# A four-layer decoder kernel: one DMA moved ahead of another in the L2 expert loop, weight loads split over two queues, the zeroing of buffer rows moved and cut

## The reference

```python
capacity = int(CAPACITY_FACTOR * T * K / E)
ranks = take_along_axis(cumsum(onehot, axis=0), flat_sel[:, None], axis=1)[:, 0] - 1
valid = ranks < capacity
slot = where(valid, flat_sel * capacity + ranks, sentinel)
padded = zeros((sentinel + 1, d)).at[slot].set(x_rep)
h = gelu(einsum('ecd,edf->ecf', padded, w1)); out_padded = einsum('ecf,efd->ecd', h, w2)
gathered = where(valid, out_padded[min(slot, sentinel - 1)], 0)
out = (gathered * weights).sum over the two choices
```

## Time and profile before

| | |
|---|---|
| median of three executions | 2066.54 us |
| the profiled execution's own time | 2069.29 us |
| its span, first to last instruction | 2067.6 us |
| PE busy | 1643.8 us (80%) |
| DVE busy | 911.0 us (44%) |
| ACT busy | 711.5 us (34%) |
| POOL busy | 436.8 us (21%) |
| moved by DMA | 37.63 MB, 18 GB/s over the span |

### The profile page before, as it was taken

One profiled execution on the slowest core, in us unless ns is written; L12 is line 12 of the kernel. 1 busy time (PEld: TensorE's weight loads), 2 busy tenths in 40 slices (PEclk: granted clock), 3 DMA queues, 4 the chain that ended last, 5 costly groups with the idle time before them and its releaser, 6 DMA issues. The chain is left out here.

```text
span 2067.6 us, 31792 instructions
## 1 busy us (share of the span) xinstructions
PE 1643.8 (80%) x11656; PEld 963.7 (47%) x11656; DVE 911.0 (44%) x2515; ACT 711.5 (34%) x1423; POOL 436.8 (21%) x517
## 2 busy tenths in 40 slices
PE   1899899994799998869899987136156999969998
PEld 1344434443444444545644435124042555548887
DVE  3455345533355654641256535311354555324444
ACT  1244424442176775524213444011041333422221
POOL 2534043400121110000053400320515434100000
PEclk8999999997999998969999998567576999969999
DMA  8200000000000000000040000011200000000000
GB/s 235 67 2 1 1 1 1 1 1 0 0 1 1 1 1 1 1 0 1 4 148 2 1 1 1 20 53 52 59 12 6 12 12 6 1 0 0 0 0 20
DMA packets 45933, 37.63 MB, mean 18 GB/s; under 512 B 3972, under 2 KB 40040, under 8 KB 45800
## 3 DMA queue, kind: packets, MB, share of 16 engines
q1 hardware_dynamic: 43752, 31.65, 5.1%
q0 software_dynamic: 2048, 4.20, 0.7%
HBM read 23.26 MB, written 12.58 MB: 17 GB/s over the span
## 5 line engine op out<-in xcount | busy, mean ns | idle before, releaser
L1309 ACT ACTIVATE scores_L_experts_L<-L3x_psL 128x512 f32<-128x512 f32 x128 | 76.4, 597 | 173.8 <-PE L3x_psL L1172 170.2
L1346 DVE CUSTOM_DVE_ANT_0 L3x_junk<-L3x_psS,L3x_mask_rows 128x256 f32<-128x256 f32 x224 | 86.4, 422 | 92.6 <-PE L3x_psS L1134 84.5
L1172 PE MATMUL L3x_psL<-identb,L3x_mask_parts 128*128 128x256 bf16 x768 | 96.2, 276 | 0.0
L2433 ACT ACTIVATE L3f_activated<-L3f_psG 128x512 f32<-128x512 f32 x72 | 43.0, 597 | 153.0 <-PE L3f_psU L2412 153.0
L2466 DVE TENSOR_TENSOR L3f_hidden<-L3f_activated,L3f_psU 128x512 f32<-128x512 f32 x72 | 49.6, 688 | 103.0 <-ACT L3f_activated L2433 103.0
L852 ACT ACTIVATE L0x_probs<-L0x_psL 128x512 f32<-128x512 f32 x96 | 52.1, 595 | 114.1 <-PE L0x_psL L665 78.9
L852 ACT ACTIVATE L2a_probs<-L2a_psL 128x512 f32<-128x512 f32 x96 | 52.1, 595 | 104.2 <-PE L2a_psL L663 69.4
L852 ACT ACTIVATE L0a_probs<-L0a_psL 128x512 f32<-128x512 f32 x96 | 52.1, 595 | 100.8 <-PE L0a_psL L663 65.0
L1154 PE MATMUL L3x_psL<-L3x_qm,ctx_T 32*128 32x512 f32 x256 | 73.7, 651 | 12.1 <-DVE L3x_mx L1346 11.6
L2398 PE MATMUL L3f_psY<-experts_L_L,L3f_hidden 128*128 128x128 f32 x576 | 76.9, 276 | 5.0 <-DVE L3f_hidden L2466 4.9
L1172 PEld LDWEIGHTS L3x_psL<-identb,L3x_mask_parts 128*128 128x128 bf16 x768 | 70.4, 98 | 21.5 <-issue 13.7
(11 more groups left out here) (768 smaller groups left out, 4025.8 us busy)
## 6 DMA issues: line engine op xcount, KB each, us to landing
packed_rows<-zeros SPq DMA_DIRECT2D x1, 4608.0 KB, 27.2
L2f_rows<-packed_rows SPq DMA_DIRECT2D x8, 320.0 KB, 3.6
unpacked_rows<-L2f_y SPq DMA_DIRECT2D x8, 320.0 KB, 2.7
experts_L_L<-in_L_ffn_w_dram SPq DMA_DIRECT2D x1, 2048.0 KB, 8.5
unpacked_rows<-zeros SPq DMA_DIRECT2D x1, 2048.0 KB, 25.1
scores_L_experts_L<-in_L_ffn_w_dram SPq DMA_DIRECT2D x1, 2048.0 KB, 7.9
L3x_mask_rows<-in_mask_Bx1xSxS_ff_dram SPq DMA_DIRECT2D x8, 256.0 KB, 2.7
experts_L_L<-n_L_ffn_expert_gate_dram SPq DMA_DIRECT2D x1, 1024.0 KB, 13.4
```

The source lines that it names most:

```text
L1172: last = nc.tensor.matmul(at[:, :, t * P:(t + 1) * P], parts[:, b % 2, i, t, u * P:(u + 1) * P], two, start=False, stop=i == PARTS - 1, sk ...
L1309: nc.scalar.activation(probs[:, half, a, k, :], psL[i % RING][:], ACT.Exp).then_inc(s_prob, 1)
L1346: last = nc.vector.tensor_tensor_reduce(out=junk[:, i, :], in0=psS[a][:, i * S:(i + 1) * S], in1=mrow[:, b % 2, t, :], scale=1.0, scalar=L ...
```

## The change

It has three parts.

1. In `slot_experts`, SP issues `load(c + 3)` ahead of the wait and store of pair c.
2. In `load_and_turn`, the loads are split: `x`, the LoRA weights, `ctx` with the int32 weights, and the rest on SP (28 DMAs); the square and router weights and four bias rows on ACT's queue (20 DMAs), ahead of ACT's copies. Four semaphores take the place of one: PE waits for the LoRA weights, then for the squares, then for `ctx`; DVE waits for `ctx`, and at its end for the rest. ACT alone copies out the first 23 transposed tiles; the last 25 are shared. The LoRA products come before the `ctx` tiles. The seven small DVE steps on index tables come before the wait for `ctx`.
3. The layer 1 expert loads and the zeroing leave this stage for SP in the L0a stage. 5120 rows of `packed` are zeroed instead of 9216, and none of `unpacked`. The gather uses new indices `home`: the slot, or row 0 where there is no room (its weight is 0). They cost one more DVE instruction for each of the two choices.

```diff
-SQUARE = ["L1_attn_Wq", ..., "L3_xattn_wo_w", "L0_attn_w_proj"]
+SQUARE = ["L0_attn_w_proj", "L1_attn_Wq", ..., "L3_xattn_wo_w"]
...
+        from_ctx = len(turns)
+        by_dve = [i >= from_ctx and i % 2 == 1 for i in range(len(turns))]
...
             def _(sp):
-                for dst, src in firsts:
-                    sp.dma_start(dst, src).then_inc(first, 16)
-                for dst, src in loads:
-                    sp.dma_start(dst, src).then_inc(loaded, 16)
-                for dst, src in late:
-                    sp.dma_start(dst, src).then_inc(w["late"], 16)
-                sp.wait_ge(zeros, 1)
-                sp.dma_start(w["packed"].rearrange("(a p) d -> p a d", p=P), w["zeros"][:].unsqueeze(1).to_broadcast([P, ROWS2 // P, D])
-                             ).then_inc(w["zeroed"], 16)
-                sp.dma_start(w["unpacked"][ROWS2 - 2 * B * S:, :].rearrange("(a p) d -> p a d", p=P),
-                             w["zeros"][:].unsqueeze(1).to_broadcast([P, 2 * NT, D])).then_inc(w["zeroed"], 16)
+                sp.dma_start(mem.x[:], dram["x"].rearrange("b (t p) d -> p (b t) d", p=P)).then_inc(first, 16)
+                for dst, src in lora_loads:
+                    sp.dma_start(dst, src).then_inc(s_lora, 16)
+                for dst, src in ctx_loads:
+                    sp.dma_start(dst, src).then_inc(s_ctx, 16)
+                for dst, src in rest:
+                    sp.dma_start(dst, src).then_inc(s_rest, 16)
...
             def _(pe):
-                pe.wait_ge(loaded, 16 * len(loads))
+                pe.wait_ge(s_lora, 16 * len(lora_loads))
                 for i, (src, dst) in enumerate(turns):
                     if i >= rings:
-                        j = i - rings
-                        pe.wait_ge((moved_act, moved_dve)[j % 2], j // 2 + 1)
+                        wait_moved(pe, i - rings)
+                    if i == lora_after:
+                        pe.wait_ge(s_square, 16 * len(square_loads))
+                    if i == from_ctx:
+                        wait_moved(pe, lora_after - 1)
+                        nc.tensor.matmul(lora[:, 0:3 * P], la_attn[:], lbT_attn[:], start=True, stop=True)
+                        nc.tensor.matmul(lora[:, 3 * P:4 * P], la_proj[:], lbT_proj[:], start=True, stop=True).then_inc(lora_done, 1)
+                        pe.wait_ge(s_ctx, 16 * len(ctx_loads))
...
             def _(act):
+                for dst, src in square_loads:
+                    act.dma_start(dst, src).then_inc(s_square, 16)
+                for dst, src in rest_act:
+                    act.dma_start(dst, src).then_inc(s_rest, 16)
                 for i, (src, dst) in enumerate(turns):
-                    if i % 2 == 0:
+                    if not by_dve[i]:
...
             def _(dve):
-                dve.wait_ge(loaded, 16 * len(loads))
+                dve.wait_ge(built, w["iotas"])
...
+                dve.wait_ge(s_ctx, 16 * len(ctx_loads))
...
 def quad_heads(...):
                     for dst, src in loads:
                         sp.dma_start(dst, src).then_inc(w["late"], 16)
+                    if clear:
+                        sp.dma_start(clear[0], clear[1]).then_inc(clear[2], 16)
...
 def slots_of_two(...):
                     steps.step(nc.vector.scalar_tensor_tensor(at[:], key[i][:], -float(capacity), rank[:], ALU.mult, ALU.add))
+                    steps.step(nc.vector.scalar_tensor_tensor(home[:, i, :], at[:, :, 0], float(E * capacity), fits[:, :, 0],
+                                                              ALU.add, ALU.mult))
...
 def slot_experts(...):
-                pool.wait_ge(w["zeroed"], 32)
+                pool.wait_ge(w["zeroed"], 16)
...
-                                                     bass.IndirectOffsetOnAxis(ap=slot[:, i, t:t + 1], axis=0)).then_inc(s_back[t // TPB], 16)
+                                                     bass.IndirectOffsetOnAxis(ap=home[:, i, t:t + 1], axis=0)).then_inc(s_back[t // TPB], 16)
...
                 for c in range(PAIRS):
+                    if c + 3 < PAIRS:
+                        load(c + 3)
                     sp.wait_ge(s_y, c + 1)
                     sp.dma_start(rows_of(unpacked, c), y[:, c % 2, :, :]).then_inc(s_store[c % 2], 16)
-                    if c + 3 < PAIRS:
-                        load(c + 3)
```

More of the change, by code:

```diff
@@ L200, in load_and_turn @@
         lora = ctx.enter_context(nc.psum_tensor("lora", [P, 4 * P], F32))
-        loaded, first, casts = sem("weights_loaded"), sem("x_loaded"), sem("dequantized")
+        first, casts = sem("x_loaded"), sem("dequantized")
+        s_lora, s_square, s_ctx, s_rest = (sem(n) for n in ("lora_loaded", "squares_loaded", "ctx_loaded", "rest_loaded"))
         built, turned, moved_act, moved_dve = sem("ident_built"), sem("turned"), sem("moved_by_act"), sem("moved_by_dve")
         lora_done, chain = sem("lora_done"), sem("prologue_chain")
-        lanes, zeros = sem("lanes"), sem("zeros_ready")
+        lanes = sem("lanes")
         lane, kind = sb("lane", [P, P], I32), sb("lane_kind", [P, 3, P], I32)
@@ L220, in load_and_turn, with wait_moved @@
         lora_after = 7
-        def square(n):
-            return dram[n]
-        firsts = [(mem.x[:], dram["x"].rearrange("b (t p) d -> p (b t) d", p=P))]
-        loads = [
+        by_dve = [i >= from_ctx and i % 2 == 1 for i in range(len(turns))]
+        act_total, dve_total = by_dve.count(False), by_dve.count(True)
+        def wait_moved(eng, i):
+            if by_dve[i]:
+                eng.wait_ge(moved_dve, by_dve[:i + 1].count(True))
+            else:
+                eng.wait_ge(moved_act, by_dve[:i + 1].count(False))
+        lora_loads = [
             (w_attn[:], dram["L0_attn_w_attn"].rearrange("(j p) d -> p j d", p=P)),
@@ L234, in load_and_turn @@
             (ffn_int[:, 2, :].rearrange("p (j d) -> p j d", d=P), dram["L0_ffn_w_up"].rearrange("(j p) d -> p j d", p=P)),
-            (wgq[:], dram["L1_xattn_Wgq"]), (wgk[:], dram["L1_xattn_Wgk"]),
+        ]
+        square_loads = [(nat[n][:], dram[n]) for n in SQUARE]
+        square_loads += [(wgq[:], dram["L1_xattn_Wgq"]), (wgk[:], dram["L1_xattn_Wgk"])]
+        square_loads += [(gate_nat[n][:], dram[n]) for n in gates]
+        rest_act = [(mem.bias[0:1, k:k + dram[n].shape[0] // P, :],
+                     dram[n].rearrange("(a j p) -> a j p", a=1, p=P)) for n, k in BIASES.items()]
+        rest = [(w["bias_cols"][:, c + j:c + j + 1], dram[n][j * P:(j + 1) * P].rearrange("(p a) -> p a", a=1))
+                for n, c in BIAS_COLUMNS.items() for j in range(dram[n].shape[0] // P)]
+        rest += [(w[n][:], dram[n]) for n in DIRECT]
+        rest += [
             (w["bgq"][:], dram["L1_xattn_bgq"].rearrange("(p a) -> p a", a=1)),
@@ L241, in load_and_turn @@
         ]
[L242 to L254 removed]
+        w["late_count"] = 0
         with nc.Block() as block:
@@ L287, in _ @@
                                                    fill=BIG, base=0, pattern=[[1, P]], channel_multiplier=-1))
-                steps.step(nc.gpsimd.iota(w["offset"][:], pattern=[[1, P]], base=P, channel_multiplier=-1))
                 tri = w["trinity"]
@@ L324, in _ @@
                 steps.step(nc.gpsimd.memset(mem.eps[:], EPS))
-                steps.step(nc.gpsimd.iota(w["desc_int"][:], pattern=[[-1, 16]], base=16, channel_multiplier=0))
-                steps.step(nc.gpsimd.iota(w["count_int"][:], pattern=[[1, GN]], base=1, channel_multiplier=0))
-                steps.step(nc.gpsimd.iota(w["token_int"][:], pattern=[[B * S, 2], [P, NT]], base=0, channel_multiplier=1))
                 steps.step(nc.gpsimd.memset(w["zeros"][:], 0.0))
-                pool.sem_inc(zeros, 1)
                 steps.step(nc.gpsimd.memset(w["nm"][:], 0.0))
@@ L385, in _ @@
                     steps.step(nc.vector.bn_aggr(mem.mv[:, t, :], mem.stats[:, t % 2, :]))
-                dve.wait_ge(loaded, 16 * len(loads))
+                dve.wait_ge(built, w["iotas"])
+                steps.step(nc.vector.tensor_copy(w["desc"][:], w["desc_int"][:]))
+                steps.step(nc.vector.tensor_copy(w["count"][:], w["count_int"][:]))
+                steps.step(nc.vector.tensor_copy(w["token"][:], w["token_int"][:]))
+                steps.step(nc.vector.tensor_scalar(w["slot_int"][:], lane[:, 0:1], GN - 1, None, ALU.bitwise_and))
+                steps.step(nc.vector.tensor_scalar(w["slot_col"][:], w["slot_int"][:], 1.0, None, ALU.add))
+                steps.step(nc.vector.tensor_scalar(w["offset"][:], w["offset"][:], 3, None, ALU.bitwise_and))
+                steps.step(nc.vector.tensor_scalar(w["same"][:], w["offset"][:], 0.0, BIG, ALU.is_gt, ALU.mult))
+                dve.wait_ge(s_ctx, 16 * len(ctx_loads))
                 for j in range(3):
```

69 lines of the change are left out of this document (30 added, 39 removed).

## The result

The changed kernel takes 2007.61 us (median of 4 runs, 2005.79 to 2014.94) against 2066.51 us for the kernel before on the same chip (4 runs, 2065.91 to 2067.85): a ratio of 0.972, 95% interval 0.970 to 0.975. The profiled execution took 2005.79 us against 2069.29, so the two traces differ by 63.5 us and the two medians by 58.9.

The account below looks back on a forecast made before the run. SP's issue stream was taken to bound the start, late loads and PE's slowed clock the expert loop. Gains 38.7 + 26.2 - 0.4 = 64.5 us from 2069.3 give 2004.8, against the median 2002 us; range 1995 to 2017.

Parts of the forecast that it names:

- 38.7 us were predicted: Layer 2 expert loop: gain from issuing the load ahead of the store, 25.4 us idle time and 13.3 us clock.
- it lands just in time: Expert loop: the load chain of about 5.1 us fits in PE's round of 5.27 us.
- The allowance of 0.3 us for missed rounds: Expert loop: 0.3 us in all added for rounds whose load misses its time.
- Rival A: Expert loop: the load is still late and PE waits each round, only part of the gain comes, 2015 us; chance 0.10.
- 26.2 us were predicted: Start: gain from split loads and moved zeroing, L0a beginning at 28.5 us instead of 54.7.
- my 10.5: Start: landing time of `x` in us, its 7.67 delayed by the whole 2.8 from sharing full DMA engines.
- The bound for slow issues: Start: if ACT's issues take 17 us, L0a begins at 31 to 32 us and the gain is 23.
- a longer L0a as a sign of being wrong: L0a stage: the prediction would be wrong if L0a takes longer than now; the moved DMAs were put at 0.
- The sum against the profiled execution: Whole kernel: 38.7 + 26.2 - 0.4 = 64.5 us gained, from 2069.3 to 2004.8 us.
- B (bytes): Start: bound by bytes, `x` or `ctx` lands late, L0a begins at 34 to 38, 2007 to 2012 us; chance 0.17.
- C (slower, by gathers of row 0): Gathers of `unpacked`: reads of row 0 queue in memory, 2074 us at 3.5 us per gather; chance 0.01.
- D (the gain is given back): L0a or a later stage gives back the start's 26 us, time about 2028 us; chance 0.04.

Follow-up runs that it names:

- fill_wait: The kernel before with 22 matmuls without a reader ahead of each of the five waiting transposes in the layer 2 expert loop: 2055.56 us, ratio 0.994.
- swap_only: The kernel before with only SP's order of load and store in the layer 2 expert loop changed: 2032.64 us, ratio 0.983.
- start_only: The changed kernel with SP's old order of load and store put back in the expert loop: 2042.44 us, ratio 0.988.
- again: The changed kernel once more with no edit, five executions: 2006.9 us, ratio 0.971.
- start_warm: The changed kernel with 20 matmuls without a reader on PE ahead of its first wait in the start: 2007.6 us, ratio 0.971.

## Why the prediction was right or wrong

**The loop: right in size and in cause.** 38.7 us were predicted and 38.8 measured. Of the two parts, waiting was put at 25.4 and measured at 26.3, the clock at 13.3 and measured at 12.5 (fill_wait). The step "it lands just in time" was right and its margin of 0.1 to 0.2 us too: it shows as one transpose 0.14 us late in the changed kernel. The allowance of 0.3 us for missed rounds was too small for a typical run, and that the first profile had none was luck: its loop of 47.8 us is the shortest of seven with one load ahead (up to 51.5, five of them 49.3 or more). A load that PE waits 1.2 to 1.9 us for costs 1.4 to 2.0 us, or 3.8 where the clock falls. Rival A is thus a small truth: not each round, but about one round in an execution, and these are the loads of 5.0 us or more, not every load at the closer spacing.

**The start: right in size, wrong in its path.** 26.2 us were predicted and 26.0 measured, L0a at 28.5 and 28.75. The steps between were off in both directions. `x` was hardly delayed (7.82 against my 10.5 and 7.67 before), so the statistics ended at 16.5 and the casts at 19.35, 2.2 us earlier than I had it. But PE, which my sum had left out, then held the shared tiles: at the slow clock its transposes come 0.21 us apart, the LoRA products stand ahead of `ctx`, and it reached `ctx` only at 20.26. PE ended the tiles at 24.8 (4.5 us instead of 3.1) and their last copy ended at 25.1 for 25.0, DVE's end was 27.3 for 27.2, and the hand-over to L0a 1.5 us for 1.25. What the early `x` gave at the first of these tiles (20.26 for 21.6), the slower tiles took again. The sum missed that a chain which gets shorter uncovers the engine beside it, PE here. ACT's issues took 9.2 us (0.79 to 9.98) for my 8.7; SP's prices held on ACT. The bound for slow issues does not add up as I wrote it: 17 us and 23 copies of 0.24 give 22.5 and not 24.8, so L0a would begin near 29.5 and not at 31 to 32. The forecast did not rest on it.

**Part 3: right within what can be told.** L0a is 0.3 us longer than before (the lead goes from 26.0 to 25.7 at L0x), beside full DMA engines. The prediction had named a longer L0a as a sign of being wrong, but this is no price of the DMAs: L0a is 0.9 us longer in swap_only, which moves none there, and 1.1 us shorter in start_only, which does. The two DVE steps, put at 0.4, cost about 0.6: the lead falls by 0.56 to 0.74 us from L2r's first matmul to the first expert transpose in eight profiles with them, and by 0.03 and 0.12 in two without.

**From the sum to the median: the step that failed.** The sum against the profiled execution came out 1.0 us off (64.5 against 63.5). In part that is luck: beside the two gains the trace loses 3.1 us between L0a and the first expert transpose and wins 1.8 behind the loop, where the sum had only the 0.4 of the DVE steps. I then took off 2.75 us because the profiled execution of before lies that much above its median, and took it that the changed kernel's runs would lie the same way. They lie the other way: its profiled execution is 1.8 us below its own median. So 2002 was predicted and 2007.6 measured, inside the range. Over the study the kernel before spread over 12 us and the changed kernel over 11, so a correction of 2.75 us from three runs was within what the runs scatter by. The late loads (1.6 to 3.8 us in five of seven profiles, none in the first) would account for part of these 4.6 us (2.75 and 1.8); the rest is not traced.

**The rivals.** B (bytes) fell with `x` at 7.82, L0a at 28.75 and a DMA share of only 0.64 from 15 to 20 us. C (slower, by gathers of row 0) fell: the gathers keep their pace, here from POOL's timeline, 1.26 us apart as in the earlier trace rows with the same 0.95 for one:

```profile
1398.67 0.95 POOL L2921 DMA_INDIRECT L2f_back_rows<-unpacked_rows,home  x1 [0.30 <-issue]
1399.93 0.95 POOL L2921 DMA_INDIRECT L2f_back_rows<-unpacked_rows,home  x1 [0.30 <-issue]
```

D (the gain is given back) fell by start_only and again, and by fill_wait, which shows the same loss with nothing moved.

## What to carry to other kernels

Look at what stands ahead of a load in its issuing queue, not only at what the load itself waits for: a store that waits for results holds back every load behind it, and a wait on PE can cost half as much again in the work that follows it. Where a stage has several chains that end close together, take the later of them after each edit; halves of such a change measured alone give less than they do together (11.6 and 6.1 against 26.0). And leave more than a round of margin to a load in a tight loop: loads took up to 4.0 us here, but one of 5.0 to 5.7 came in seven of nine profiles of the new order, and PE did not wait for it in the two with the wider margin.

## What the runs showed of the hardware that I had not expected

- Landings scatter in two groups. A load of 320 KB took at most 4.0 us from issue to landing in 62 cases and 5.0 to 5.7 in eight, and in each of the eight a 16 KB packet of queue 8, of kind `instruction`, began in that time. Whether the packet is the cause was not tried, and stays open.
- PE's clock held through waits of 1.45 and 1.83 us in the loop (transposes behind them at 0.77 and 0.76 us) and had fallen after one of 1.90 (1.12) and after one of 2.38 in the start.
- The column of the granted clock reads 1.00 from 10 to 15 us, where the pace of the transposes shows the slow clock (0.87 us for three, 0.55 once work had gone before). From 15 to 20 us it reads 1.00 in the changed kernel and 0.50 in start_warm, while both take 1.62 us for the same LoRA product. In the first stretch of an execution the pace is the better witness.
- A semaphore step of POOL's own came before indirect DMAs queued ahead of it had run: 16 matmuls released by it began at 1320.84 us, and the two scatters behind that step ran at 1336.11 and 1337.37.
- A second issuing queue, beginning in the same microsecond as `x`'s, delayed the first use of `x` by 0.7 us in the mean (7.82 to 8.68 in nine profiles against 7.41 to 7.67 in five), with a DMA share of 1.17 from 5 to 10 us.
